# Stage joins, result stores, row buffers, load order and product order in an attention and MLP kernel

## The chip, the cores and the metric

One NeuronCore of a Trainium2 chip runs the whole program. The metric is the device time of one execution in microseconds. Engines are named PE (TensorE), PEld (its weight loads), DVE (VectorE), ACT (ScalarE), POOL (GpSimd) and SP (SyncE), which only issues transfers here.

## What is computed

```python
xn = layernorm(x)                                   # x is (16, 512, 128)
x + causal_attention(xn) + ffn(xn)

# causal_attention: 16 heads of 64, relative position bias, softmax, @ Wo + bo
# ffn: two layers, each
h = shift_token(x)                                  # second half of the features from the row before
q, k, v = split(h @ wqkv)                           # 8 heads of 64; l2norm, scales, rotary
x = x + local_attention(q, k, v) @ wo               # windows of 64, one window back
h = layernorm(shift_token(x)) * lg + lb
a, g = split(h @ w1 + b1)                           # 2 x 341
x = x + (a * gelu(g)) @ w2 + b2
```

All inputs and results are f32. Most products are made of three f32r passes (high and low parts of both operands).

## The kernel before

The normalised input and later the residual of `ffn` stay on chip in `xf` (64 tiles of 128 rows). There are 16 batches of 4 tiles.

`causal_attention` runs first: 16 batches times 8 pairs of heads, one slot (b, p) for each, with an order of work written out by hand for each engine. POOL scales the probabilities, ACT makes exponentials and copies, DVE adds the bias table and makes the low parts, PE multiplies and transposes. At p = 4 the next batch is transposed too (`transpose_x`, `xT_high` on ACT, `xT_low` on DVE), before k of the next pair is projected. Each finished batch is stored to `out` from SP's queue; the program waits for the last store.

`transformer` then opens a block of its own: SP loads the rotary table and layer 0's weights, the shifted rows of batch 0 (`load_shifted`, up to three copies a tile, chip to chip memory) and reads `out` back to `f_acc` (4 MB). POOL builds masks. Then comes a hardware loop over the two layers; its body is `local_attention` and `gated_mlp`, each a block whose engines meet at its end.

`local_attention` has 64 tiles, one slot (b, t) each, and a pipeline of up to five slots. It begins with DVE's split of `wqkv` and POOL's scaling of the tables (`f_tab`). In slot (b, t) SP waits until the place in `f_hs` is free, copies the tile's shifted rows, and then copies `f_v` of two tiles back to `f_vm`. PE transposes the rows (L1149) near the end of the same tile's slot; ACT makes `f_hT_hi` and DVE `f_hT_lo`. At the end SP copies the shifted rows of batches 0 and 1 for the MLP.

`gated_mlp` has 16 slots of a batch of 512 rows and three more to drain. SP starts with the next layer's attention weights, then copies each batch's shifted rows into one of two buffers with three copies (L745 to L747), after the batch two before has been normalised. In slot b DVE normalises batch b - 1, gates batch b - 2 (`gated(0)`), takes the statistics of batch b, adds the result of batch b - 3 to `xf` and gates twice more. PE makes the products of `w1` (`hidden`), the transposes, and the products of `w2` (`second`). POOL makes the reciprocal root and `hT_lo`. After its last slot SP copies the shifted rows of batch 0 for the next layer.

After the loop DVE adds `xf` to `f_acc` in four parts, and SP stores them.

Of the kernel before, what the change touches and what calls it, by code (L numbers as in the profile page):

```python
# [112 lines left out]
def causal_attention(nc, c, x, Wq, Wk, Wv, Wo, bo, rel, out, ext_dram):  # L113

    xf, ident, bank = c["xf"], c["ident"], c["bank"]
    with ExitStack() as ctx:
# [101 lines left out]
        def _(sp):  # L218
# [20 lines left out]
            def turn(b, par):  # L239

                if not isinstance(b, int) or b < B - 2:
                    sp.wait_ge(s_Ya, at(b, HP, 2))
                    sp.dma_start(xb[:, par], xv[:, bass.ds(b * TT + 2 * TT, TT), :]).then_inc(s_x[par], 16)
                for half in range(2):
                    sp.wait_ge(s_Ya, at(b, HP, 7 + half))
                    sp.dma_start(ov[:, bass.ds(b * TT + 2 * half, 2), :],
                                 yacc[:, 2 * half:2 * half + 2, :]).then_inc(s_out[half], 16)
            for b in range(B):
                turn(b, b % 2)
            for half in range(2):  # L250
                sp.wait_ge(s_out[half], 16 * B)

        @block.gpsimd
        def _(pool):
# [39 lines left out]
            def slot(b, p, par):  # L294
# [15 lines left out]
                if p == 4 and has_scores(b) and has_next(b):  # L310
                    keep(b + 1, 1 - par)
            pair_slots(pool, slot, 1)

        @block.scalar
        def _(act):
# [39 lines left out]
            def slot(b, p, par):  # L355
# [52 lines left out]
        def _(dve):  # L408
# [51 lines left out]
            def slot(b, p, par):  # L460
# [37 lines left out]
                logits(3, 0)  # L498
                if step is not None:
# [9 lines left out]
                if p == 4 and has_scores(b) and has_next(b):  # L509
                    xT_low(b + 1, 1 - par)  # L510
# [244 lines left out]
def load_attention_weights(eng, c, d, l, s):  # L755

    def row(a):
        return a[bass.ds(l, 1), :].to_broadcast([P, DH])
    eng.dma_start(c["wqkv"][:], d["wqkv"][bass.ds(l, 1), :, :].squeeze(0)).then_inc(s, 16)
    eng.dma_start(c["wo4"][:], d["wo"][bass.ds(l, 1), :, :].squeeze(0).rearrange("(c p) n -> p c n", p=P)).then_inc(s, 16)  # L760
    eng.dma_start(c["qk_scale"][:, 0, :], row(d["q_scale"])).then_inc(s, 16)
    eng.dma_start(c["qk_scale"][:, 1, :], row(d["k_scale"])).then_inc(s, 16)


def local_attention(nc, c, d, l, w):
# [17 lines left out]
    def _(sp):  # L783

        s = sem["weights"]
        sp.dma_start(c["w1"][:], d["w1"][bass.ds(l, 1), :, :].squeeze(0)).then_inc(s, 16)
        sp.dma_start(c["w2"][:, 0:2, :], d["w2"][bass.ds(l, 1), 0:2 * P, :].squeeze(0).rearrange("(c p) n -> p c n", p=P)).then_inc(s, 16)
        sp.dma_start(c["w2"][0:CH[2], 2, :], d["w2"][bass.ds(l, 1), 2 * P:HID, :].squeeze(0)).then_inc(s, 16)
        sp.dma_start(c["w2"][CH[2]:CH[2] + 1, 2, :], d["b2"][bass.ds(l, 1), :]).then_inc(s, 16)
        with nc.allow_non_contiguous_dma(reason="a few columns, once a layer"):  # L790
            sp.dma_start(c["ln"][:, 0:1], d["ln_g"][bass.ds(l, 1), :].rearrange("l p -> p l")).then_inc(s, 16)
            sp.dma_start(c["ln"][:, 1:2], d["ln_b"][bass.ds(l, 1), :].rearrange("l p -> p l")).then_inc(s, 16)
            for part in range(2):
                for j in range(3):
# [4 lines left out]
        def slot(b, t):
            if not isinstance(b, int) or 0 < b < B:  # L800
# [4 lines left out]
            if two is not None:  # L805
# [16 lines left out]
    def _(pool):  # L822
        for n in w["mlp"].values():
            pool.sem_clear(n)

        for k in range(4):
            nc.gpsimd.tensor_tensor(tab[:, :, k, :], w["rope"][:, :, k, :],
                                    c["qk_scale"][:, k // 2, :].unsqueeze(1).to_broadcast([P, TT, DH]),
                                    ALU.mult).then_inc(sem["tab"], 1)
# [4 lines left out]
        def slot(b, t):  # L834
# [21 lines left out]
            if one is not None:  # L856
# [6 lines left out]
                nc.gpsimd.tensor_tensor(rn[:, r, :], ssq[:, r, :], w["mhalf"][:], ALU.pow).then_inc(sem["rn"], 1)  # L863
        tile_slots(pool, slot)

    @block.scalar
    def _(act):
        def slot(b, t):
# [21 lines left out]
            def rotated_out(k):  # L890
# [620 lines left out]
```

## Time and profile before

| | |
|---|---|
| three runs | 2701.99, 2704.53, 2706.19 us |
| median | 2704.53 us |
| profiled execution | 2707.02 us |
| its span | 2705.2 us |
| PE, PEld busy | 2547.8 us (94%), 1988.1 us (73%) |
| ACT, DVE, POOL busy | 2158.3 (80%), 2009.4 (74%), 1629.7 us (60%) |
| mean granted clock of PE | 0.977 |
| transfers | 77.07 MB, mean 28 GB/s |

The span reaches from the first to the last instruction; the execution's own time lies around it. Busy shares are means over stages with different limits. In timelines "[2.81 <-DMA f_hs<-xf]" is the engine's idle time before the group and what ended it; "SPq" is SP's queue, and its duration that of issuing, not of the transfer.

### The profile page before, as it was taken

What the parts mean: (1) busy time and instruction counts of PE and PEld (TensorE: products, weight loads), DVE (VectorE), ACT (ScalarE), POOL (GpSimd) and SP (SyncE); (2) the same over time, 40 slices, a digit from 0 to 9 for tenths busy, and PEclk for the clock granted to TensorE, in tenths of its full rate; (3) what the DMA queues carried; (4) which work ended last, traced back from release to release, by engine and by line L of the source; (5) the groups of instructions that cost most, each with busy time, mean ns of one, the idle gap of its engine ahead of it and who ended that gap; (6) DMA issues with size and microseconds to landing.
All of it is one profiled execution on the core that took longest, in us unless ns stands there. A gap on an engine that the chain in (4) does not pass through costs nothing. (4 is left out here: it accounts for less than half of the span.)

```text
span 2705.2 us, 71234 instructions
## 1 busy us (share of the span) xinstructions
PE 2547.8 (94%) x24208; PEld 1988.1 (73%) x24208; DVE 2009.4 (74%) x5647; ACT 2158.3 (80%) x6335; POOL 1629.7 (60%) x1947
## 2 busy tenths in 40 slices
PE   7999999999999999999599999997979999999796
PEld 4777777777777777777378888885767888888575
DVE  4666666666666666666389999995659999999565
ACT  5888888888888888888389999996438999999642
POOL 3444444444444444444389999994229999999521
PEclk8999999999999999999799999998989999999898
DMA  2000000000000000000311111111111111111112
GB/s 72 7 7 10 9 9 5 8 7 9 9 9 5 10 7 7 9 6 5 103 41 41 38 42 39 38 42 46 33 26 40 38 42 42 38 40 42 46 33 79
DMA packets 128513, 77.07 MB, mean 28 GB/s; under 512 B 80196, under 2 KB 110736, under 8 KB 128144
## 3 DMA queue, kind: packets, MB, share of 16 engines
q1 hardware_dynamic: 127968, 72.34, 10.9%
q8 instruction: 199, 3.26, 0.5%
q14 instruction: 170, 1.39, 0.2%
q10 hardware_dynamic: 176, 0.07, 0.0%
HBM read 17.58 MB, written 8.41 MB: 10 GB/s over the span
## 5 line engine op out<-in xcount | busy, mean ns | idle before, releaser
L306 POOL TENSOR_SCALAR L<-L,rinv 128x128 f32<-128x128 f32 (+3 forms) x1024 | 522.4, 533 | 622.7 <-DVE rinv L488 622.7
L370 ACT ACTIVATE L<-L,nmax 128x384 f32<-128x384 f32 (+3 forms) x1024 | 571.8, 561 | 144.2 <-DVE nmax L474 144.2
L474 DVE CUSTOM_DVE_ANT_0 L<-bank,bias_tab 128x256 f32<-128x256 f32 (+3 forms) x1024 | 470.5, 479 | 180.3 <-PE bank L590 178.3
L886 ACT ACTIVATE f_L<-bank,f_nmax,f_rn 128x128 f32<-128x128 f32 x1024 | 459.9, 486 | 5.0 <-DVE f_nmax L1013 5.0
L863 POOL TENSOR_TENSOR f_rn<-f_ssq,f_mhalf 128x16 f32<-128x16 f32 x128 | 419.1, 3274 | 18.2 <-DVE f_ssq L997 4.7
L845 POOL TENSOR_TENSOR f_qkr<-f_ab 128x256 f32<-128x256 f32 x512 | 414.3, 838 | 10.3 <-DVE f_ab L964 10.3
L611 PE MATMUL bank<-ident,L 128*128 128x128 f32 x2560 | 370.4, 276 | 2.3 <-DVE PT L215 2.0
L611 PEld LDWEIGHTS bank<-ident,L 128*128 128x128 f32 x2560 | 296.8, 141 | 83.4 <-issue 46.1
L964 DVE TENSOR_TENSOR f_ab<-bank,f_tab 128x512 f32<-128x512 f32 x512 | 347.8, 680 | 8.8 <-ACT f_sq L876 8.8
L632 PE MATMUL bank<-PT,v 128*64 128x512 f32 (+3 forms) x2048 | 303.9, 439 | 0.6 <-DVE yacc L507 0.4
L632 PEld LDWEIGHTS bank<-PT,v 128*64 128x64 f32 x2048 | 126.8, 136 | 166.2 <-issue 164.9
L886 ACT ACTIVATION_READ_ACCUMULATOR f_L<-bank,f_nmax,f_rn 128x1 f32 x1024 | 239.6, 234 | 0.0
L215 ACT ACTIVATE PT<-bank 128x512 f32<-128x512 f32 x384 | 226.9, 591 | 6.2 <-PE bank L611 4.2
L443 DVE TENSOR_TENSOR k_lo<-bank,k_hi 128x512 fp32r<-128x512 f32 x128 | 88.5, 691 | 187.8 <-ACT k_hi L337 187.8
L215 DVE COPY PT<-bank 128x512 f32<-128x512 f32 x256 | 175.6, 686 | 36.1 <-PE bank L611 35.9
L370 ACT ACTIVATION_READ_ACCUMULATOR L<-L,nmax 128x1 f32 x1024 | 201.8, 197 | 0.0
L1050 PE MATMUL bank<-f_w_hi,f_hT_hi 128*128 128x512 f32 x384 | 188.1, 490 | 10.5 <-DVE f_hT_lo L1026 10.5
L988 DVE TENSOR_REDUCE f_rmax<-bank 128x4 f32<-128x512 f32 x256 | 164.8, 685 | 30.9 <-PE bank L1083 30.9
L590 PE MATMUL bank<-k_hi,q_hi 64*128 64x128 f32 (+3 forms) x1024 | 180.1, 348 | 6.3 <-DVE k_lo L443 5.3
L876 ACT ACTIVATE f_sq<-bank 128x512 f32<-128x512 f32 x256 | 174.2, 681 | 12.9 <-PE bank L1052 12.9
L978 DVE TENSOR_REDUCE f_ssum<-f_sq 128x8 f32<-128x512 f32 x256 | 169.5, 662 | 0.0
L590 PE MATMUL bank<-k_hi,q_lo 64*128 64x128 f32 (+3 forms) x1024 | 166.0, 320 | 0.0
(145 smaller groups left out, 6390.8 us busy)
## 6 DMA issues: line engine op xcount, KB each, us to landing
f_vm<-f_v SPq DMA_DIRECT2D x224, 128.0 KB, 2.4
f_hs<-xf SPq DMA_DIRECT2D x132, 32.0 KB
f_hs<-xf SPq DMA_DIRECT2D x132, 31.8 KB
xb<-in_L_attn_x SPq DMA_DIRECT2D x16, 256.0 KB, 2.8
out<-yacc SPq DMA_DIRECT2D x32, 128.0 KB, 1.8
f_hs<-xf SPq DMA_DIRECT2D x32, 128.0 KB
out<-f_acc SPq DMA_DIRECT2D x4, 1024.0 KB, 7.5
f_hs<-xf SPq DMA_DIRECT2D x32, 127.0 KB
```

The costliest lines, as they stand in the source:

```text
L215: copy(PT[:, k, 0:n], ps_t[(h + k) % 2][:, 0:n], *how).then_inc(s_C[engine], 1)
L306: nc.gpsimd.tensor_scalar(t, t, rinv[:, h % RING, a, i:i + 1], 1.0, ALU.mult, ALU.mult).then_inc(s_N, 1)
L370: nc.scalar.activation(t, t, ACT.Exp, bias=nmax[:, ep % RING, a, i:i + 1], scale=-1.0, accum_out=rsum[:, ep % RING, a, i:i + 1]).then_inc( ...
L474: nc.vector.tensor_tensor_reduce(out=L[:, p % RING, a, LOFF[i]:LOFF[i] + (i + 1) * P], in0=ps_s[a][i], in1=bias_tab[:, 2 * p + a, T - (i + ...
L590: last[a] = nc.tensor.matmul(ps_s[a][i], qq[row, r, tok], kk[row, r, keys], start=(n == 0), stop=(n == 2))
L611: last = nc.tensor.transpose(ps_t[(h + k) % 2][:, n * P:n * P + P], L[:, h % RING, a, LOFF[i] + j * P:LOFF[i] + j * P + P], ident[:])
L632: last = nc.tensor.matmul(ps_o[DH * a:DH * a + DH, j * P:T], v[:, j, head:head + DH], PT[:, fill, off:off + T - j * P], start=(j == 0), st ...
L845: nc.gpsimd.tensor_tensor(halves(qkr[:, tt % 2, k], s), halves(ab[:, tt % 2, k, 0], s), halves(ab[:, tt % 2, k, 1], 1 - s), ALU.add).then_inc(
L863: nc.gpsimd.tensor_tensor(rn[:, r, :], ssq[:, r, :], w["mhalf"][:], ALU.pow).then_inc(sem["rn"], 1)
L886: nc.scalar.activation(L[:, ot % 2, a, k, :], ps_s[a][:, k * P:k * P + P], ACT.Exp, bias=nmax[:, ot % 2, a, k:k + 1], scale=rn[:, ot % 2, ...
L964: ins = nc.vector.tensor_tensor(ab[:, it % 2, k, n, :].rearrange("p (h e) -> p h e", h=FH), src[:].rearrange("p (h e) -> p h e", h=FH), ta ...
L1050: nc.tensor.matmul(ps[:], hT_hi[:, it % 2, :], w_hi[:, col], start=True, stop=False)
```

## The change

Six things change.

1. *Joins.* `transformer_start` allocates part of the layers' tensors ahead of the causal attention; some of them are places in that stage's tensors (`f_rows` is its bias table). At (0, 6) POOL builds the masks; at b = 1 SP copies the shifted rows of batch 0; at b = 15, after pair 3, SP loads table and weights of layer 0; POOL scales and splits them at (15, 6), (15, 7) and (16, 0). The block between is gone; some fills open layer 0 on POOL. The loop over the layers is written out. In `local_attention` the first batch of the MLP is taken through statistics, scale, transposes and affine step, and `w1` is split, in the last slots. In the MLP of layer 0 POOL prepares the weights of layer 1.
2. *Results.* `out` is read back at slot (6, 0) of layer 0's attention. In the last MLP, POOL adds `xf` to `f_acc` batch by batch, DVE adds the batch's result to that, and ScalarE's queue stores it, 256 KB each, in the slot after.
3. *Buffers.* Four buffers for the MLP's shifted rows instead of two (two lie in `f_sq`). Batches 0 and 1 are copied at slots (4, 0) and (5, 0) of the attention.
4. *Loads.* In layer 0's MLP SP issues the next layer's tables and weights in slots 4 to 6 and the shifted rows of its batch 0 in slots 7 to 10. The last MLP loads nothing of that kind.
5. *Products.* PE does `hidden(0)`, `hidden(1)`, the transposes, all of `second`, `hidden(2)`. DVE adds the result after `gated(1)`.
6. *p = 4 of the causal attention.* ACT copies `v` before the exponential (2, 1); DVE makes `xT_low` before it adds to `yacc`.

```diff
 # causal_attention, SP
             def turn(b, par):
+                if b == B - 1:
+                    sp.wait_ge(s_L, at(b, 8 * HP, 8 * 4))
+                    for part in range(3):
+                        load_attention_weights(sp, c, d, w, 0, part, w["s_load"])
+                if b == 1:
+                    sp.wait_ge(s_xf, 1)
+                    sp.wait_ge(w["s_hs_zero"], 1)
+                    for t in range(TT):
+                        load_shifted(sp, c["hs"], xf, 0, t, w["attn"][f"hs{t}"])
...
 # causal_attention, POOL
+                if (b, p) == (0, 6):
+                    build_masks(nc, pool, c, w)
+                for n in {(B - 1, 6): (0, 1, 2), (B - 1, 7): (3, 4, 5), (B, 0): (6, 7)}.get((b, p), ()):
...
+                    prepare_attention(nc, pool, c, w, n, w["s_load"])
 # causal_attention, ACT
                 fills(1)
+                if p == 4 and item is not None:
+                    value_out(item)
                 exps(2, 1)
-                if item is not None:
+                if p != 4 and item is not None:
                     value_out(item)
 # causal_attention, DVE
                 logits(3, 0)
+                if p == 4 and has_scores(b) and has_next(b):
+                    xT_low(b + 1, 1 - par)
                 if step is not None:
...
-                if p == 4 and has_scores(b) and has_next(b):
-                    xT_low(b + 1, 1 - par)
                 logits(0, 0)

-def load_shifted_batch(sp, hs, xf, b, r, s_hs):
-    x_b = xf[:, bass.ds(b * TT, TT), :]
+def load_shifted_batch(sp, w, xf, b):
+    hs, s_hs = w["shifted"][b % 4], w["mlp"][f"hs{b % 4}"]
+    x_b = xf[:, b * TT:b * TT + TT, :]
     half = D // 2
-    sp.dma_start(hs[:, r, :, 0:half], x_b[:, :, 0:half]).then_inc(s_hs, 16)
-    sp.dma_start(hs[1:P, r, :, half:D], x_b[0:P - 1, :, half:D]).then_inc(s_hs, 16)
-    sp.dma_start(hs[0:1, r, 1:TT, half:D], x_b[P - 1:P, 0:TT - 1, half:D]).then_inc(s_hs, 16)
+    sp.dma_start(hs[:, :, 0:half], x_b[:, :, 0:half]).then_inc(s_hs, 16)
+    sp.dma_start(hs[1:P, :, half:D], x_b[0:P - 1, :, half:D]).then_inc(s_hs, 16)
+    sp.dma_start(hs[0:1, 1:TT, half:D], x_b[P - 1:P, 0:TT - 1, half:D]).then_inc(s_hs, 16)

+def load_attention_weights(eng, c, d, w, l, part, s):
+    if part == 0:
+        eng.dma_start(w["tab"], d["rope"].rearrange("(t p) k e -> p t k e", p=P)).then_inc(s, 16)
+    elif part == 1:
+        eng.dma_start(w["w_raw"], d["wqkv"][l]).then_inc(s, 16)
+    else:
+        # wo and two rows of scales
+def prepare_attention(nc, pool, c, w, n, s_loaded):
+    # n = 0..3: a quarter of the tables; 4..7: high and low parts of wqkv, 1024 and 512 columns
+def batch_statistics(nc, dve, w, b):      # as in the MLP before: bn_stats, bn_aggr, add epsilon
+def batch_scale(nc, pool, w, b):          # rstd
+def batch_normalise(nc, dve, w, b):       # hn
+def batch_transposes(nc, pe, c, w, b):    # four transposes to bank 6
+def batch_affine(nc, act, c, w, b):       # mT and mT_hi
+def batch_low(nc, pool, w, b):            # mT_lo

 # local_attention, SP, at the end of slot(b, t); the two loads after the slots are gone
+            if b in (4, 5) and t == 0:
+                sp.wait_ge(w["s_fill"], 4)
+                sp.wait_ge(sem["x_out"], 2 * TT)
+                load_shifted_batch(sp, w, xf, b - 4)
+            if (l, b, t) == (0, 6, 0):
+                sp.dma_start(w["acc"][:], d["out"].rearrange("b (t p) d -> p (b t) d", p=P)).then_inc(w["s_acc"], 16)
 # local_attention: DVE (B, 0) statistics of 0, (B, 2) normalise 0 and statistics of 1;
 # POOL (B, 1) scale, (B, 2) split of w1, (B + 1, 0) low; PE (B, 3) transposes; ACT (B + 1, 0) affine

 # gated_mlp, SP
-        load_attention_weights(sp, c, d, 1 - l, sem["weights"])
+        nxt = l + 1 if l < DEPTH - 1 else None
         def slot(b, r):
-            if isinstance(b, int) and (b < 2 or b >= B):
-                return
-            sp.wait_ge(sem["hn"], at(b, TT, -TT))
-            load_shifted_batch(sp, hs, xf, b, r, sem[f"hs{r}"])
+            if 2 <= b < B:
+                sp.wait_ge(sem["hn"], at(b, TT, -3 * TT))
+                load_shifted_batch(sp, w, xf, b)
+            if nxt is not None and 4 <= b < 7:
+                load_attention_weights(sp, c, d, w, nxt, b - 4, sem["weights"])
+            if nxt is not None and 7 <= b < 11:
+                sp.wait_ge(sem["x_out"], 1)
+                load_shifted(sp, c["hs"], xf, 0, b - 7, w["attn"][f"hs{b - 7}"])
 # gated_mlp, POOL
+            if l == DEPTH - 1 and now is not None:
+                pool.wait_ge(w["s_acc"], 16)
+                a = w["acc"][:, b * TT:b * TT + TT, :]
+                nc.gpsimd.tensor_tensor(a, a, xf[:, b * TT:b * TT + TT, :], ALU.add).then_inc(sem["acc"], 1)
 # gated_mlp, ACT, ahead of gelu(0)
+            four = batch_back(b, 4)
+            if l == DEPTH - 1 and four is not None:
+                act.wait_ge(sem["x_out"], four + 1)
+                act.dma_start(d["out"].rearrange("b (t p) d -> p (b t) d", p=P)[:, four * TT:four * TT + TT, :],
+                              w["acc"][:, four * TT:four * TT + TT, :]).then_inc(w["s_stored"], 16)
 # gated_mlp, PE
             hidden(0)
+            if two is not None:
+                pe.wait_ge(sem["H"], at(two, 3, -1))
+            hidden(1)
+            if one is not None and one > 0:
+                batch_transposes(nc, pe, c, w, one)
             if three is not None:
                 pe.wait_ge(sem["H"], at(three, 3, 3))
                 pe.wait_ge(sem["x_out"], at(three, 1, 0))
-                second(range(2))
-            # transposes of batch `one`
-            if three is not None:
-                second(range(2, TT)).then_inc(sem["y_done"], 1)
+                second()
             if two is not None:
                 pe.wait_ge(sem["H"], at(two, 3, 0))
-            hidden(1)
             hidden(2)
 # transformer
-        with nc.Fori(0, DEPTH) as l:
+        for l in range(DEPTH):
             local_attention(nc, c, d, l, w)
             gated_mlp(nc, c, d, l, w)
-        # a block before the loop (loads, masks) and one after it (four sums, four stores)
```

## Rows read from the trace of the kernel before

**Rows 1.** Windows by stage: start:end, us, busy of each engine, granted clock, DMA.
```profile
1315.60:1342.00 26.40, 0.52 (x2) 0.22 (x2) 5.32 (x6) 1.56 (x2) 7.71 (x16) 0.52 0.49 143
1342.00:1865.70 523.70, 511.47 (x6399) 424.00 (x6399) 479.47 (x1023) 493.12 (x1599) 481.44 (x384) 0.98 0.19 44
1865.70:2010.20 144.50, 123.77 (x736) 101.34 (x736) 81.14 (x272) 57.28 (x81) 39.08 (x34) 0.95 0.15 36
2010.20:2020.20 10.00, 0.47 (x1) 0.18 (x1) 3.58 (x3) 1.56 (x2) 4.28 (x4) 0.63 0.25 62
...
2685.70:2705.20 19.50, 0.00 (x0) 0.00 (x0) 8.92 (x5) 0.00 (x0) 0.00 (x0) 0.57 0.76 215
```

**Rows 2.** Timeline of the first join: start, us, engine, line, idle before it.
```profile
1315.13 0.42 DVE L507 TENSOR_TENSOR yacc<-bank,yacc 128x256 f32<-128x256 f32 x1 [1.31 <-PE bank L655]
1318.67 0.11 POOL L1411 MEMSET f_mhalf<- 128x16 f32 x1 [14.45 <-POOLq L116]
...
1339.01 0.48 PE L1149 MATMUL bank<-ident,f_hs 128*128 128x128 f32 x1 [23.92 <-DVE f_w_lo L942]
1339.53 0.28 ACT L913 ACTIVATE f_hT_hi<-bank 128x128 fp32r<-128x128 f32 x1 [2.02 <-PE bank L1149]
1341.62 0.29 DVE L1026 TENSOR_TENSOR f_hT_lo<-bank,f_hT_hi 128x128 fp32r<-128x128 f32 x1 [2.66 <-POOL f_tab L827]
...
1341.96 0.80 PE L1050 MATMUL bank<-f_w_hi,f_hT_hi 128*128 128x512 f32 x1 [2.47 <-DVE f_hT_lo L1026]
```

**Rows 3.** Timeline of the MLP, layer 0: SyncE's issues and the statistics.
```profile
1939.95 6.53 SPq L747 DMA_DIRECT2D f_hs<-xf  x1
...
1946.52 0.66 SPq L745 DMA_DIRECT2D f_hs<-xf  x1
...
1947.22 0.71 SPq L746 DMA_DIRECT2D f_hs<-xf  x1
...
1948.67 0.87 DVE L1265 BATCH_NORM_STATS2 f_stats<-f_hs 128x6 f32<-128x128 f32 x4 [2.81 <-DMA f_hs<-xf]
```

**Rows 4.** Timeline of the end.
```profile
2685.04 0.69 DVE L1276 TENSOR_TENSOR xf<-bank,xf 128x512 f32<-128x512 f32 x1 [3.04 <-PE bank L1302]
...
2688.55 9.66 SPq L1453 DMA_DIRECT2D out<-f_acc  x4
```

**Rows 5.** Timeline of the MLP's start, layer 0.
```profile
1874.21 0.66 SPq L745 DMA_DIRECT2D f_hs<-xf  x1
...
1875.39 0.78 ACT L1225 ACTIVATE f_mT<-bank,f_ln 128x512 f32<-128x512 f32 x1 [11.26 <-PE bank L1319]
...
1876.99 1.26 POOL L1202 TENSOR_TENSOR f_w_lo<-f_mT,f_w_hi 128x512 fp32r<-128x512 f32 x1 [3.96 <-ACT f_w_hi L1228]
```

**Rows 6.** Timeline of steady attention: a tile's rows, and the transpose using them.
```profile
1494.35 0.60 SPq L734 DMA_DIRECT2D f_hs<-xf  x1
...
1495.65 0.86 SPq L738 DMA_DIRECT2D f_hs<-xf  x1
...
1503.90 0.27 PE L1149 MATMUL bank<-ident,f_hs 128*128 128x128 f32 x1
```

**Rows 7.** Timeline of SyncE in the first join.
```profile
1334.04 0.85 SPq L1396 DMA_DIRECT2D f_acc<-out  x1
...
1336.39 11.52 SPq L786 DMA_DIRECT2D f_w<-in_L_ffn_w  x1
```

**Rows 8.** Timeline of a causal slot with p = 4.
```profile
707.51 0.40 PE L527 MATMUL bank<-wv_lo,xT_hi 128*128 128x512 f32 x1
...
707.95 0.60 ACT L345 ACTIVATE v<-bank 128x512 f32<-128x512 f32 x1
...
709.30 0.59 ACT L330 ACTIVATE xT_hi<-bank 128x512 fp32r<-128x512 f32 x1
...
710.52 0.68 DVE L437 TENSOR_TENSOR xT_lo<-bank,xT_hi 128x512 fp32r<-128x512 f32 x1
...
711.26 0.50 PE L525 MATMUL bank<-xT_hi,wk_hi 128*128 128x512 f32 x1 [0.68 <-DVE xT_lo L437]
```

More of the change, by code:

```diff
@@ L251, in _ @@
                 sp.wait_ge(s_out[half], 16 * B)
+            sp.wait_ge(w["s_load"], 16 * 5)
+            for t in range(TT):
+                sp.wait_ge(w["attn"][f"hs{t}"], shifted_count(t))
         @block.gpsimd
@@ new lines, in batch_statistics @@
+def batch_statistics(nc, dve, w, b):
+    sem, hs, stats, mv, ve = w["mlp"], w["shifted"][b % 4], w["stats"], w["mv"], w["ve"]
+    dve.wait_ge(sem[f"hs{b % 4}"], 48 * (b // 4 + 1))
+    for t in range(TT):
+        nc.vector.bn_stats(stats[:, t, :], hs[:, t, :]).then_inc(sem["stats"], 1)
+    dve.wait_ge(sem["stats"], at(b, TT, TT))
+    dve.wait_ge(sem["hn"], at(b, TT, 0))
+    dve.sem_inc(w["gate_dve"], 1)
+    for t in range(TT):
+        nc.vector.bn_aggr(mv[:, t, :], stats[:, t, :]).then_inc(sem["mv"], 1)
+    dve.wait_ge(sem["mv"], at(b, TT, TT))
+    nc.vector.tensor_scalar(ve[:], mv[:, :, 1], LN_EPS, None, ALU.add).then_inc(sem["ve"], 1)
@@ new lines, in batch_scale @@
+def batch_scale(nc, pool, w, b):
+    pool.wait_ge(w["mlp"]["ve"], b + 1)
+    nc.gpsimd.tensor_tensor(w["rstd"][:], w["ve"][:], w["mhalf"][:, 0:TT], ALU.pow).then_inc(w["mlp"]["rstd"], 1)
+def batch_transposes(nc, pe, c, w, b):
+    sem, ps_t = w["mlp"], c["bank"][6]
+    pe.wait_ge(sem["hn"], TT * (b + 1))
+    pe.wait_ge(sem["hT_hi"], b)
+    for t in range(TT):
+        last = nc.tensor.transpose(ps_t[:, t * P:t * P + P], w["hn"][:, t, :], c["ident"][:])
+    last.then_inc(sem["T_done"], 1)
@@ new lines, in batch_low @@
+def batch_low(nc, pool, w, b):
+    sem = w["mlp"]
+    pool.wait_ge(sem["hT_out"], b + 1)
+    pool.wait_ge(sem["hT_hi"], b + 1)
+    nc.gpsimd.tensor_tensor(w["mT_lo"][:, b % 2, :], w["mT"], w["mT_hi"][:, b % 2, :].bitcast(F32),
+                            ALU.subtract).then_inc(sem["hT_lo"], 1)
+def batch_normalise(nc, dve, w, b):
+    sem = w["mlp"]
+    dve.wait_ge(sem["rstd"], b + 1)
+    dve.wait_ge(sem["T_done"], b)
+    for t in range(TT):
+        nc.vector.tensor_scalar(w["hn"][:, t, :], w["shifted"][b % 4][:, t, :], w["mv"][:, t, 0:1], w["rstd"][:, t:t + 1],
+                                ALU.subtract, ALU.mult).then_inc(sem["hn"], 1)
@@ L822, in _ @@
     def _(pool):
[L823 to L829, printed above, removed]
+        if l > 0:
+            for n in w["mlp"].values():
+                pool.sem_clear(n)
+        else:
+            nc.gpsimd.memset(kT[:, :, 0:WIN], 0.0).then_inc(w["s_fill"], 1)
+            nc.gpsimd.memset(vm[0:WIN, 0, :], 0.0).then_inc(w["s_fill"], 1)
+            nc.gpsimd.memset(w["hs2"][:], 0.0).then_inc(w["s_fill"], 1)
+            nc.gpsimd.memset(w["Hh"][:, :, 2, :], 1.0).then_inc(w["s_fill"], 1)
         def halves(a, r):
@@ L1183, in _ @@
-        for t in range(TT):
-            sp.wait_ge(w["attn"][f"hs{t}"], shifted_count(t))
-        sp.wait_ge(sem["weights"], 64)
+            if 2 <= b < B:
[6 more added lines that the diff above has]
+                load_shifted(sp, c["hs"], xf, 0, b - 7, w["attn"][f"hs{b - 7}"])
@@ L1207, in _ @@
+            if now is not None and b > 0:
+                batch_scale(nc, pool, w, b)
+            if l < DEPTH - 1 and 7 <= b < 15:
+                prepare_attention(nc, pool, c, w, b - 7, sem["weights"])
+            if l == DEPTH - 1 and now is not None:
+                pool.wait_ge(w["s_acc"], 16)
+                a = w["acc"][:, b * TT:b * TT + TT, :]
+                nc.gpsimd.tensor_tensor(a, a, xf[:, b * TT:b * TT + TT, :], ALU.add).then_inc(sem["acc"], 1)
         batch_slots(pool, slot, 3)
@@ L1295, in hidden, with second @@
                     nc.tensor.matmul(ps[0:n, :], w1_hi[:, col], hT_lo[:, r, :], start=False, stop=True).then_inc(sem["ga_done"], 1)
-            def second(tiles):
-                for t in tiles:
+            def second():
+                for t in range(TT):
                     for j in range(3):
@@ L1310, in slot @@
             hidden(0)
+            if two is not None:
+                pe.wait_ge(sem["H"], at(two, 3, -1))
+            hidden(1)
+            if one is not None and one > 0:
+                batch_transposes(nc, pe, c, w, one)
             if three is not None:
@@ L1313, in slot @@
                 pe.wait_ge(sem["x_out"], at(three, 1, 0))
-                second(range(2))
-            if one is not None:
-                pe.wait_ge(sem["hn"], at(one, TT, TT))
-                pe.wait_ge(sem["hT_hi"], at(one, 1, 0))
-                for t in range(TT):
-                    last = nc.tensor.transpose(ps_t[:, t * P:t * P + P], hn[:, t, :], ident[:])
-                last.then_inc(sem["T_done"], 1)
-            if three is not None:
-                second(range(2, TT)).then_inc(sem["y_done"], 1)
+                second()
             if two is not None:
                 pe.wait_ge(sem["H"], at(two, 3, 0))
-            hidden(1)
             hidden(2)
```

312 lines of the change are left out of this document (151 added, 161 removed).

## The prediction

> **What bounds the kernel now.** I read the stretches between the stages' ends first [rows 1]. An attention layer (523.7 us) keeps PE 98% and ACT 94% busy. An MLP (144.5 us) does not: PE works 123.8 us, ACT 57.3, POOL 39.1. Three stretches hold almost no compute: 26.4 us between the causal attention and the first attention layer, 10.0 us between the layers, 19.5 us at the end.
>
> Then the timeline, to see what fills them. In the first join [rows 2] the last addition ends at 1315.55, the first transpose comes at 1339.01, held by DVE's split of the weights, and the first projection at 1341.96, since `hT_lo` stood in DVE's stream behind a wait for POOL's tables. In the MLP [rows 3] VectorE waits 2.81 us at `bn_stats` for a load. SyncE issues the three copies of a batch in 0.66, 0.71 and 6.53 us, and the next batch's first follows the third's end by 0.04 us: 1939.95 + 6.53 = 1946.48, then 1946.52. So SyncE doesn't wait for a free buffer there; it is full, and its 8.02 us a batch (third copy to third copy: 1939.95, 1947.97) are the MLP's cadence.
>
> **The joins.** *Causal attention to layer 0.* Weights, tables, masks and shifted rows are made earlier. The barrier stays: 3.12 us from the last addition to the next block's first instruction, 1318.67 [rows 2]. Then transpose to `hT_hi` 0.52, `hT_hi` itself 0.28, from `hT_lo`'s start to the projection 0.34, and 0.2 to start with: 1320.1. Gain 21.9 us (20 to 22.5). POOL's four fills there lie beside transposes, projections and DVE's products, before its first rotation; if that cover is gone they cost their 2.5 us or so, which is in the bound. The preparation that moves under the last pairs of the causal stage runs on POOL between its shares of those pairs; at the very tail I allow 0.4 us, an estimate.
>
> *Between the layers* [rows 1] 10.0 us become the same start and a table load of ACT, 2.5 us: gain 7.5 (6 to 8.5).
>
> *End.* The last addition ends at 2685.73, after which come 19.5 us of sums and four 1 MB stores [rows 1, 4]. One store of 256 KB remains. Store, landing and barrier of the causal stage took 3.12 us [rows 2]; with twice the bytes 3.2. Gain 16.3 (15 to 17). This execution took 2707.02 us, its span and 1.8 us, and is 2.5 us above the median of the runs; the difference is applied to the median, 2704.53.
>
> **The MLP stages.** The first load inside the MLP is issued at 1874.21 [rows 5], because it must wait for batch 0's `hn`; the stage began at 1865.7. With four buffers SyncE starts at once: 8.3 us earlier in each layer, 16.5 in both. That the first product also comes earlier does not count: from the third batch on `bn_stats` waits for SyncE. The form of the three copies is unchanged, so 14 batches still take 14 x 8.02 = 112.3 us. Before, 1874.21 + 112.3 + 2.2 of landing (1946.48 to 1948.67) is 1988.7, and the stage ended 21.5 us later; these are products of the last batches, the same number in the new order, so they stay. PE's 123.8/16 = 7.7 us a batch would be next, only 0.3 us below SyncE.
>
> Now what is added to that full stream. In layer 0 SyncE issues the next layer's loads inside slots 4 to 10. Four `load_shifted` take 2.16 us each (1494.35 to 1496.51 [rows 6]): 8 us. Weights and tables are 1.6 MB; four 1 MB stores took from 2688.55 to 2705.2 [rows 1, 4], 252 GB/s, by which these are 6 us of everything that copies, or 2 us if only issuing counts. I take 5: 13 us together (8 to 14). Before, they lay ahead of or behind the batches. In layer 1 twelve stores of 256 KB run before the last load lands; at that rate 1.04 us each. Only ScalarE's queue issues them, so either the copying is what is full (12 us) or SyncE's own time (0). I take 11 (0 to 12), since an issue of 6.53 us for the smallest of three copies [rows 3] reads as a queue that is held up by the copy before it.
>
> The Trainium skill (DMA: Bandwidth & Descriptors, "Why a DMA increments its semaphore by 16 and not by 1") says that 127 partitions put a whole copy on one DMA engine; the second copy of a batch has 127, and the trace's 6.53 us behind it agree. The same page ("Issuing engines are not separate DMA queues") speaks against the stores: another issuing engine brings no bandwidth. By it they cost their 11 us; if SyncE's time alone were the bound, 0, and the sum would be 2676.
>
> **New waits in the attention layers.** There the next tile's shifted rows are issued from 1494.35, the last of them until 1496.51, and transposed at 1503.90 [rows 6]. With 2.2 us of landing the slack is 5.2 us; PE and ACT are full, so what is later than that is lost. (a) The copies of MLP batches 0 and 1 now stand in SyncE's stream at slots (4,0) and (5,0), ahead of the next tile's rows: 8.0 us [rows 3] less 5.2 is 2.8 us, four times in two layers: 11 us (0 to 18). Behind the late rows stand PE's `values()`, ACT's `hT_hi` and with them all of the slot. (b) The 4 MB read of `out` moves to slot (6,0). Before, it was issued at 1334.04 and SyncE was stuck behind it until 1347.91, in an issue of 11.52 us [rows 7]: 13.9 us in place of the 0.60 of an issue, so 13.3 - 5.2 = 8.1 us lost once (2 to 12).
>
> **The rest.** Batch 0's statistics, transposes and affine step go into the attention's tail. After the last copy of `OT` ACT makes two steps of 0.78 us and POOL one of 1.26 [rows 5] before the barrier, partly beside the last product: 1.5 us a layer (1 to 2.5), 3 in all. The granted clock of PE was 0.52 in the first join [rows 1], that is the lower of its two levels, and full in the steady stage; with less idle time at the joins I give back 2 us (0 to 5). In the causal stage PE waits 0.68 us for `xT_lo` at p = 4 [rows 8], 15 times. `xT_lo` starts at 710.52 though `xT_hi` ended at 709.89, because the `yacc` addition stands first; moving it up is worth up to 0.6 us. But ACT's copy of `v` starts at 707.95, 0.04 us after PE's product (707.51 + 0.40), beside which an exponential of 0.6 us ran; pulled ahead of it the copy starts no earlier, and the exponential then delays `xT_hi`. The two cancel: 0 (-8.5 to +8).
>
> **The sum.** Gains 21.9 + 7.5 + 16.3 + 16.5 + 2 = 64.2. Losses 13 + 11 + 11 + 8.1 + 3 + 0.4 = 46.5. Net 17.7 us less: 2704.5 - 17.7 = 2686.8, say 2687.
>
> **Rivals.** *A: the new loads and stores are hidden.* Rows arrive in time and stores fit between. For it: copying is busy only 15 to 19% of the engines' time in these stages [rows 1]; against: SyncE's full cadence. Without 11 + 8 + 11 the net is -48, 2657; with half of it 2672. *B, on the other side: a long copy holds up the tile loads for its whole length.* If rows behind a batch copy come 9 us too late and those behind the read of `out` 16, that is 52 us instead of 19, and the net is +15: 2720. It decides from 37 us on, 7 us a batch copy with 9 for the read. For it: the third copy is held for 6.53 us; against: the batch copy after it starts without further delay. *C: four buffers free the MLP.* Then PE's 7.7 us set it: 28 x 0.3 = 8 us less, and 24 of the additions gone: 2655. *D: the joins don't shrink*, since a block starts as slowly unrolled as looped: the 7.5 and some 6 of the 21.9 are lost, 2700.
>
> **How the numbers follow.** My own sum, net -6 to -30: 0.55. A 0.20, C 0.07, B 0.10, D or a mixture near zero 0.08. Within 0.2%, 5.4 us, this measurement can hardly tell a change. Faster is 0.55 + 0.20 + 0.07 = 0.82, the same 0.08, slower 0.10. The range, 2662 to 2704, leaves out B and the far halves of A and C; the likeliest case's own is 2675 to 2699.
>
> **What would show it.** Right: the first projection near 1320; `bn_stats` still waiting for a load every 8.0 us, and every 9 in the second MLP; the transposes of `f_hs` late by 3 us at tiles 17 and 21 of each layer and by 8 at tile 25 of the first; 3 us after the last addition; PE's wait for `xT_lo` still there. Wrong: a third copy that is issued quickly, an MLP slot of 7.7 us, attention slots of 7.8 us throughout, or transposes late by more than 7 us each time.

## The result, and the profile after

The changed kernel takes 2709.73 us (median of 17 runs, 2706.78 to 2713.74), the kernel before 2704.53 in the same job: ratio 1.0019, 95% interval 1.0011 to 1.0026. The forecast was 2687 us. The change makes the kernel 5 us slower, just below what I had called the limit of telling; the interval lies wholly above 1.

The profiled execution after has a span of 2711.2 us. These are its windows by stage, with the columns of [rows 1].

```profile
1316.06:1320.96 4.90, 0.45 (x2) 0.19 (x2) 0.29 (x1) 0.28 (x1) 1.40 (x3) 0.58 0.19 43
1320.96:1872.92 551.96, 521.22 (x6403) 430.15 (x6403) 486.85 (x1045) 496.44 (x1601) 485.64 (x389) 0.96 0.19 45
1872.92:2025.30 152.38, 127.82 (x732) 102.64 (x732) 79.02 (x252) 54.22 (x79) 43.52 (x39) 0.96 0.16 37
2025.30:2026.83 1.53, 0.30 (x1) 0.14 (x1) 0.29 (x1) 0.28 (x1) 0.00 (x0) 0.99 0.24 23
2026.83:2565.93 539.10, 516.57 (x6403) 426.76 (x6403) 486.36 (x1045) 497.37 (x1602) 485.29 (x387) 0.97 0.17 39
2565.93:2708.50 142.57, 123.00 (x732) 100.53 (x732) 82.63 (x253) 54.22 (x79) 55.84 (x47) 0.98 0.21 54
2708.50:2711.20 2.70, 0.00 (x0) 0.00 (x0) 0.00 (x1) 0.00 (x0) 0.00 (x0) 1.00 0.33 97
```

Set beside the same stretches of before, with the prediction's terms put to the stage where they act:

| stretch, span us | before | after | measured | predicted |
|---|---|---|---|---|
| causal attention, to its last addition | 1315.56 | 1316.06 | +0.5 | +0.4 |
| first join, to the first projection | 26.40 | 4.90 | -21.5 | -21.9 |
| attention, layer 0, to its last addition | 523.71 | 551.96 | +28.3 | +15.1 |
| MLP, layer 0 | 144.51 | 152.38 | +7.9 | +4.8 |
| join between the layers | 10.05 | 1.53 | -8.5 | -7.5 |
| attention, layer 1 | 521.61 | 539.10 | +17.5 | +7.0 |
| MLP, layer 1 | 143.89 | 142.57 | -1.3 | +2.8 |
| end | 19.45 | 2.72 | -16.7 | -16.3 |
| clock given back | | | (in the rows) | -2.0 |
| sum | 2705.18 | 2711.22 | +6.0 | -17.7 |

The joins gave what was forecast: 46.7 us against 45.7. The attention layers took 45.8 us where 22.1 were forecast, and that is the miss. Their loss has three places. First, the slots behind a batch copy. SyncE's queue and PE's transpose of the tile's rows, in the timeline of the changed kernel (line 768 is the first copy of a batch, 770 the third, 756 the first of a tile):

```profile
1443.11 6.47 SPq L770 DMA_DIRECT2D f_hs<-xf  x1
1449.63 0.52 SPq L756 DMA_DIRECT2D f_hs<-xf  x1
...
1453.93 0.47 PE L1301 MATMUL bank<-ident,f_hs 128*128 128x128 f32 x1 [2.66 <-DMA f_hs<-xf]
```

And the 4 MB read (line 950) with the issue held behind it, the first copy of tile 25's rows:

```profile
1514.59 0.84 SPq L950 DMA_DIRECT2D f_acc<-out  x1
1515.49 14.15 SPq L756 DMA_DIRECT2D f_hs<-xf  x1
```

And windows from transpose to transpose: a normal slot, the one that ends with this wait, the two behind it, then the two after the 4 MB read.

```profile
1435.40:1443.26 7.86, 7.86 (x103) 6.54 (x101) 7.48 (x18) 7.70 (x27) 7.59 (x7) 1.00 0.20 47
1443.26:1453.93 10.67, 8.01 (x103) 6.46 (x101) 8.13 (x18) 8.29 (x29) 9.49 (x9) 0.97 0.18 42
1453.93:1464.54 10.61, 10.61 (x101) 8.84 (x101) 6.80 (x16) 7.35 (x23) 6.39 (x5) 0.71 0.15 34
1464.54:1472.28 7.74, 7.74 (x102) 6.50 (x101) 7.36 (x18) 7.69 (x27) 5.97 (x6) 1.00 0.19 43
...
1515.90:1533.78 17.88, 8.03 (x103) 6.46 (x101) 8.15 (x18) 8.29 (x29) 9.49 (x9) 0.85 0.91 248
1533.78:1543.77 9.99, 9.99 (x101) 8.42 (x101) 6.80 (x16) 7.34 (x23) 6.38 (x5) 0.75 0.13 31
```

The reader is to see two different losses of 2.8 us. In the second row PE works its usual 8.0 us and waits 2.7. In the third nothing waits, PE is busy for all of 10.61 us with the work that it does in 7.8 elsewhere: the granted clock is 0.71, which is the lower of its two levels for 6.3 us of that slot. A batch copy costs 2.8 + 2.8 us (1.45 instead of the second 2.8 where the low clock lasts 3.4 us), 9.8 a layer; the 4 MB read 10.0 + 2.2.

Second, the tail of the attention. DVE, POOL and PE there (894 is the normalisation of the MLP's batch 0, 841 the statistics of batch 1, 1148 the product that makes the last tile's probabilities, 1005 and 1007 the split of `w1`), and below it the view of line 894 alone:

```profile
1859.85 3.72 DVE L894 TENSOR_SCALAR f_hn<-f_hs,f_mv,f_rstd 128x128 f32<-128x128 f32 x4
1863.49 0.86 DVE L841 BATCH_NORM_STATS2 f_stats<-f_hs 128x6 f32<-128x128 f32 x4
...
1865.22 0.69 DVE L1148 TENSOR_TENSOR f_L<-f_L,f_rinv 128x512 f32<-128x512 f32 x1
...
1860.02 1.07 POOL L991 TENSOR_TENSOR f_L<-f_L,f_rinv 128x512 f32<-128x512 f32 x1 [4.92 <-DVE f_rinv L1099]
1861.03 0.75 POOL L1005 CAST f_w_hi<-f_w 128x682 fp32r<-128x682 f32 x1
1861.87 1.63 POOL L1007 TENSOR_TENSOR f_w_lo<-f_w,f_w_hi 128x682 fp32r<-128x682 f32 x1
...
1865.97 1.12 PE L1248 MATMUL bank<-ident,f_L 128*128 128x128 f32 x4 [4.18 <-DVE f_L L1148]
```

```profile
L894 DVE TENSOR_SCALAR f_hn<-f_hs,f_mv,f_rstd x4: 333/920/1786, 1859.9 to 1861.8; 128x128 f32<-128x128 f32 x4
```

Four operations of 0.33 us on a free DVE take 3.72; beside POOL's three the slowest takes 1.79. PE waits 4.18 us for a product that stands in DVE's stream behind them. In the kernel before, the wait for the same product was 0.71 us:

```profile
1858.90 0.93 PE L1096 MATMUL bank<-ident,f_L 128*128 128x128 f32 x4 [0.71 <-DVE f_L L1002]
```

From the last tile's transpose to the last addition the tail grew from 32.76 to 38.65 us and from 31.45 to 37.33: 5.9 in each layer.

Third, a steady attention slot is 7.852 us where it was 7.834: some 2 us in all.

In the second MLP a batch now takes 8.42 us, SyncE still without a gap. The rows that answer to [rows 3]:

```profile
2601.99 6.93 SPq L770 DMA_DIRECT2D f_sq<-xf  x1
...
2608.97 0.65 SPq L768 DMA_DIRECT2D f_sq<-xf  x1
2609.66 0.70 SPq L769 DMA_DIRECT2D f_sq<-xf  x1
...
2611.77 0.87 DVE L841 BATCH_NORM_STATS2 f_stats<-f_sq 128x6 f32<-128x128 f32 x4 [2.93 <-DMA f_sq<-xf]
```

### The profile page after: what moved, and what is told of

The parts are those of the page before. It is cut to its first block and busy times, and to the rows that moved or that the text cites. A ratio compares the mean times of both kernels' runs of the same rounds, so it can differ in the third digit from the quotient of the medians.

```text
span 2711.2 us, 71091 instructions
## 1 busy us (share of the span) xinstructions
PE 2567.7 (95%) x24208; PEld 1999.8 (74%) x24208; DVE 2005.6 (74%) x5640; ACT 2157.7 (80%) x6334; POOL 1662.2 (61%) x1974
## 5 line engine op out<-in xcount | busy, mean ns | idle before, releaser
L496 DVE CUSTOM_DVE_ANT_0 L<-bank,f_rows 128x256 f32<-128x256 f32 (+3 forms) x1024 | 469.7, 478 | 179.2 <-PE bank L612 177.3
L982 POOL TENSOR_TENSOR f_qkr<-f_rows 128x256 f32<-128x256 f32 x512 | 413.4, 837 | 28.3 <-DVE f_rows L1110 28.3
L1110 DVE TENSOR_TENSOR f_rows<-bank,f_rows 128x512 f32<-128x512 f32 x512 | 347.5, 679 | 16.4 <-ACT f_sq L1023 16.4
L991 POOL TENSOR_TENSOR f_L<-f_L,f_rinv 128x512 f32<-128x512 f32 x128 | 133.4, 1042 | 66.6 <-DVE f_rinv L1099 50.7
L1055 ACT ACTIVATE f_PT<-bank 128x512 f32<-128x512 f32 x256 | 139.4, 595 | 37.4 <-PE bank L1248 31.4
## 6 DMA issues: line engine op xcount, KB each, us to landing
f_hs<-xf SPq DMA_DIRECT2D x128, 31.8 KB
```

The source lines that it names most:

```text
L496: nc.vector.tensor_tensor_reduce(out=L[:, p % RING, a, LOFF[i]:LOFF[i] + (i + 1) * P], in0=ps_s[a][i], in1=bias_tab[:, 2 * p + a, T - (i + ...
L982: nc.gpsimd.tensor_tensor(halves(qkr[:, tt % 2, k], s), halves(ab[:, tt % 2, k, 0], s), halves(ab[:, tt % 2, k, 1], 1 - s), ALU.add).then_inc(
L1110: ins = nc.vector.tensor_tensor(ab[:, it % 2, k, n, :].rearrange("p (h e) -> p h e", h=FH), src[:].rearrange("p (h e) -> p h e", h=FH), ta ...
```

## The experiments

All but one start from the changed kernel. Times are medians; the ratio is to the kernel before on the same chip, and for comparison that of the changed kernel is 1.0019 (1.0011 to 1.0026).

### The 127-partition copy in two

```diff
-    sp.dma_start(hs[1:P, :, half:D], x_b[0:P - 1, :, half:D]).then_inc(s_hs, 16)
+    cut = P - 16
+    sp.dma_start(hs[1:cut + 1, :, half:D], x_b[0:cut, :, half:D]).then_inc(s_hs, 16)
+    sp.dma_start(hs[cut + 1:P, :, half:D], x_b[cut:P - 1, :, half:D]).then_inc(s_hs, 16)
```

(The counts that wait for a batch go from 48 to 64.)

> The changed kernel, but in each batch load the copy of 127 partitions (rows 1 to 127 of the second half) is issued as two copies, of 112 and of 15 partitions; one more DMA a batch, the bytes are the same. Theory: the 127-partition copy is served by too little of the DMA hardware, so that the third copy's issue (6.5 us on SyncE's queue in the profile of the changed kernel) stands behind it. Then that issue falls below 1 us, both MLPs run at TensorE's own pace (12 + 6 products of 0.23 us, 24 of 0.12, transposes: about 7.6 us a batch against 8.42 in the second MLP and 7.8 to 10.9 in the first), which gives about 20 and 10 us, and the late tiles 17, 18, 21 and 22 of the attention (10.7, 10.6, 10.6, 9.3 us against 7.86, in both layers) disappear, which gives about 18: near 2662 against 2710. Rival 1, the bytes or the number of pieces set it: one more issue of 0.7 us per batch and no gain, 2708 to 2720. Rival 2, SyncE's issues are relieved but something else holds the MLP at 8 us: only attention and the extra loads gain, about 30 us, 2680.

2649.5 us (2646.26 to 2650.52), ratio 0.9796 (0.9779 to 0.9812). The theory holds in all its places, and the gain of 60 us is larger than the 48 that I expected, chiefly because a batch of either MLP takes 7.28 us and not 7.6. SyncE's queue and the statistics in the second MLP (768, 770, 771, 772 are now a batch's four copies):

```profile
2559.47 0.68 SPq L768 DMA_DIRECT2D f_sq<-xf  x1
...
2560.19 0.66 SPq L770 DMA_DIRECT2D f_sq<-xf  x1
2560.89 0.90 SPq L771 DMA_DIRECT2D f_sq<-xf  x1
...
2561.83 0.74 SPq L772 DMA_DIRECT2D f_sq<-xf  x1
...
2567.30 0.86 DVE L843 BATCH_NORM_STATS2 f_stats<-f_hs 128x6 f32<-128x128 f32 x4
```

No issue is held, and the statistics no longer wait for a load (no bracket behind the row). The rates of DMA in 40 us of the second MLP, each number the mean of 1 us, first of the changed kernel (2600 to 2640 us), then of this one (2560 to 2600 us):

```profile
GB/s 25 45 117 18 18 18 18 220 62 36 138 23 18 18 18 108 176 25 83 78 18 18 18 18 241 41 37 137 23 18 18 18 156 126 19 117 43 18 18 18
```

```profile
GB/s 49 180 41 1 0 246 16 0 184 87 8 0 171 91 0 130 118 15 0 94 169 0 82 161 18 1 9 253 0 29 176 72 1 0 216 47 0 144 116 2
```

The plateaus of 18 GB/s, three or four microseconds long in every batch, are the 127-partition copy with nothing else beside it (with other transfers on top it lasts longer: 127 KB at 18 GB/s are 7.2 us). The next expectation misreads this row where it says that DMA moved 18 GB/s for 6.5 us of a batch: it is three or four, and the 6.5 us are the length of the held issue. With the cut they are gone. MLP stages: 124.8 and 123.1 us (152.4 and 142.6); attention: the late tiles 17, 18, 21 and 22 are at 7.8 or 7.9 us in both layers.

### Which cut: 113 + 14, and 126 + 1

The same edit with `cut = P - 15` and with `cut = P - 2`.

> As x1_copy_split, but cut at 113 and 14 partitions instead of 112 and 15. Theory 1: how a copy is spread over the 16 DMA engines hangs on whether its number of partitions can be divided (127 and 113 are prime, 112 = 16 x 7; the Trainium skill, page DMA: Bandwidth & Descriptors, has a rule of this kind). The sum goes by the trace: in the MLP of the changed kernel the DMA moved 18 GB/s for some 6.5 of every 8.4 us with a sixteenth of the engines busy. Then 113 partitions stay on one engine, 113/127 of 7.2 us = 6.4 us, an issue behind it on SyncE is still held for 5 us or more, tiles 17 and 21 stay late, a slot with extra loads stays above 8 us: 2665 to 2695. Theory 2: any cut into two smaller copies does it: 2649.5, as with 112 and 15.

> As x1_copy_split, but cut at 126 and 1 partitions. Theory 1 (the divisor; 126 = 14 x 9): nearly the whole copy is spread, over 14 engines: 2649 to 2653, as with 112 and 15. Theory 2 (the size of the largest piece counts): 126 partitions are as good as 127, nothing is gained and an issue is added: 2708 to 2720.

113 + 14: 2707.83 us, ratio 1.0002 (0.9986 to 1.0017). 126 + 1: 2648.51 us, ratio 0.9778 (0.9738 to 0.9819). One partition more in the first copy than in the cut above takes nearly the whole gain away, and a copy of 126 is as good as one of 112. So the size of the copy does not decide; the number's divisors fit. The view of line 771, the issue behind the copy of 113 partitions:

```profile
L771 SPq DMA_DIRECT2D f_sq<-xf x16: 5682/5782/7659, 1874.4 to 2673.1; - x16
```

Its median is 5.78 us, where the third copy of the changed kernel takes 6.6 to 6.9 and the same line behind 112 partitions 0.91. I had put the time of this kernel at 2665 to 2695; that was wrong, since the copy is 11% shorter but the issue added costs 0.75 us, and SyncE is as full as before (7.9 to 8.3 us a batch in the second MLP). The Trainium skill (DMA: Bandwidth & Descriptors, "Why a DMA increments its semaphore by 16 and not by 1") gives the largest number up to 16 that divides the partitions as the number of engines that share a copy; by it that is 1 for 127 and 113, 16 for 112, 14 for 126. The three cuts agree. They don't tell this rule from a simpler one, such as any even number, for which an odd number with divisors would have to be tried; but two engines for 126 partitions don't fit, since the rates with 126 + 1 show no plateau either.

### The kernel before with the same cut

```diff
-    sp.dma_start(hs[1:P, r, :, half:D], x_b[0:P - 1, :, half:D]).then_inc(s_hs, 16)
+    cut = P - 16
+    sp.dma_start(hs[1:cut + 1, r, :, half:D], x_b[0:cut, :, half:D]).then_inc(s_hs, 16)
+    sp.dma_start(hs[cut + 1:P, r, :, half:D], x_b[cut:P - 1, :, half:D]).then_inc(s_hs, 16)
```

> The kernel before with the split copy alone. Theory: the two MLPs of the kernel before were bound by the same copy (8.02 us a batch), not by TensorE, and two buffers are enough: they fall to the 7.28 us of the changed kernel with the split copy, 2 x 14 x 0.74 = 21 us: 2684. Then the change without the queue trouble is worth 2684 - 2649.5 = 34 us. Rival: with two buffers the load waits for the normalisation two batches back, and the load's whole time (three issues, landing) shows: 7.6 us or more a batch, 2692 to 2704.

2682.01 us (2680.91 to 2686.81), ratio 0.9924 (0.9910 to 0.9937). With two buffers a batch takes 7.29 us, so four are not needed for the cadence. The change itself is worth 32.5 us from here (2682.0 to 2649.5). Rival C (2655) took the buffers for what held the MLP. It was the copy: the changed kernel has the four buffers and took 2710 us, and that 2655 lies near the 2649.5 of the kernel with the cut is luck.

### The read of the output in pieces, and on another queue

```diff
-            if (l, b, t) == (0, 6, 0):
-                sp.dma_start(w["acc"][:], d["out"].rearrange("b (t p) d -> p (b t) d", p=P)).then_inc(w["s_acc"], 16)
+            if l == 0 and b < B and t == 1:
+                n = b * TT
+                sp.dma_start(w["acc"][:, n:n + TT, :],
+                             d["out"].rearrange("b (t p) d -> p (b t) d", p=P)[:, n:n + TT, :]).then_inc(w["s_acc"], 16)
```

> The changed kernel, but the 4 MB read of the output back into f_acc is 16 reads of 256 KB, one per batch, each at the second tile of the batch in the first layer's attention. Theory: the one long read holds the tile loads behind it (one attention interval of 17.9 us and one of 10.0 against 7.86), and 256 KB fit into the slack of a tile: 12 us less, 2697.5. Rival: the bytes cost what they cost wherever they are, each piece delays its tile by 0.75 us: 2709 to 2711.

2699.36 us, ratio 0.9981 (0.9972 to 0.9991). The first attention layer falls from 552.0 to 537.8 us, and the two long intervals are 7.9. The rival is out: the same bytes in pieces cost nothing.

The other kernel leaves the read whole, and at its place in the order, but has `act.dma_start` in place of `sp.dma_start`.

> The changed kernel with the 4 MB read in one piece at the same place, but issued by ScalarE and not by SyncE. Theory 1: the read held the tile loads because they stood behind it on SyncE's queue (one issue of 14.15 us after it), and the hardware behind both queues takes them in turns: the interval of 17.9 us falls to 9 or 10 and the time to 2698 to 2702. Theory 2: the read fills what both queues share, tile loads are late whoever issues it: 2708 to 2712.

2704.5 us, ratio 1.0002 (0.9992 to 1.0011): between the two. Timeline, ACT's issue (1081), SyncE's third copy of a tile (760), PE's transpose:

```profile
1524.29 0.86 ACTq L1081 DMA_DIRECT2D f_acc<-out  x1
...
1524.47 0.87 SPq L760 DMA_DIRECT2D f_hs<-xf  x1
...
1533.00 7.15 SPq L760 DMA_DIRECT2D f_hs<-xf  x1
...
1545.92 0.48 PE L1301 MATMUL bank<-ident,f_hs 128*128 128x128 f32 x1 [4.55 <-DMA f_hs<-xf]
```

The tile copy beside the read passes, and so do the next tile's first two; the third of the next tile is held for 7.15 us, where on SyncE's queue the very next issue was held for 14.15. PE waits 4.55 us instead of 9.85. But the hold ends at nearly the same distance from the read: 15.9 us after its issue here (1524.29 to 1540.15), 15.1 us in the changed kernel (1514.59 to 1529.64). So the other queue did not shorten what holds SyncE; it let five issues through first, and the one that is held came later. How much of the hold belongs to the queue itself this run doesn't show. The low clock behind the wait costs 2.9 us (2.2 in the changed kernel).

### The order of the tail

```diff
-            if (b, t) == (B, 2):
+            if (b, t) == (B, 3):
                 batch_normalise(nc, dve, w, 0)
                 batch_statistics(nc, dve, w, 1)
```

> The changed kernel, but the normalisation of batch 0 and the statistics of batch 1 stand one slot later in VectorE's order, behind the product of the last tile's probabilities. Theory: in the attention's tail TensorE waits 4.2 us for that product, which is queued behind 3.72 us of normalisation and 1.5 us of statistics; with the order changed about 4 of the 5.9 us that each tail has grown by come back, once in each layer: 2702. Rival, the normalisation is only late elsewhere (TensorE's transposes of its result then end later by as much, before the same last addition): 2708 to 2712.

2701.75 us, ratio 0.9990 (0.9981 to 1.0000). The tails are 34.89 and 33.77 us (38.65 and 37.33); PE's wait of 4.18 us for the product is 0.71:

```profile
1859.85 0.69 DVE L1148 TENSOR_TENSOR f_L<-f_L,f_rinv 128x512 f32<-128x512 f32 x1
...
1863.09 1.11 DVE L894 TENSOR_SCALAR f_hn<-f_hs,f_mv,f_rstd 128x128 f32<-128x128 f32 x4
...
1860.59 0.66 PE L1248 MATMUL bank<-ident,f_L 128*128 128x128 f32 x4 [0.71 <-DVE f_L L1148]
```

Behind POOL's work the four operations take 1.11 us together, 0.34 each. The remaining 2.2 us a tail are open. Two things lie in them whose shares no run separates: the added work (four transposes on PE, 0.66 us, and the steps around them), and a granted clock that is still lower than before, 0.90 against 0.95 in layer 0's tail and 0.95 against 1.00 in layer 1's.

### Without the stores

The issue in ScalarE's stream is made only for the last batch (`four == B - 1`), so 15 of 16 batches of the output are not written. ScalarE's waits ahead of these stores go with them.

> The changed kernel, but 15 of the 16 batches of the result are not stored (only the last one is), so that its output is not the reference's. Theory: the stores and their waits on ScalarE's queue are what makes a batch of the second MLP 8.42 us where one without extra loads took 7.8 to 8.1 in the first: about 0.45 x 13 = 6 us less, 2704. Rival: SyncE's three issues (0.66 + 0.7 + 6.6, and gaps) set 8.42 and the stores are hidden: no change, 2709 to 2711.

2705.64 us, ratio 1.0002 (0.9993 to 1.0012). A batch of the second MLP takes 8.08 us on average instead of 8.42, the stage 138.35 instead of 142.57: the stores, with those waits, cost 4.2 us. In the kernel with the cut nothing of that is seen: its second MLP, with stores, takes the same 7.28 us a batch as its first.

### All three together, and half of the reorder at p = 4

The cut at 112 + 15, the read in 16 pieces and the tail's new order, in one kernel.

> The changed kernel with three edits together: the 127-partition copy of a batch split in 112 and 15, the read of the output in 16 pieces, the tail's order on VectorE. If they add up: 2649.5 - 14 (attention of the first layer with the pieces: 537.8 us against 552.0) - 7.3 (tails 3.8 and 3.6 us shorter) = 2628. If the pieces of the read cost the same again once the copies no longer hold the queue, or the tail's 4 us are given back at the start of a faster MLP: 2635 to 2642.

2625.66 us (2624.86 to 2628.54), ratio 0.9714 (0.9701 to 0.9727). They add up, 2 us better than the sum. On top of it:

```diff
-                if p == 4 and item is not None:
-                    value_out(item)
                 exps(2, 1)
-                if p != 4 and item is not None:
+                if item is not None:
                     value_out(item)
```

> The kernel x5_three with ScalarE's order in slot p = 4 of the causal attention put back (the value copy after the exponentials), VectorE's move left in. The step in the prediction gave VectorE's move alone 0.57 us less in each of 15 slots (11.57 us now), 8.5 us less than x5_three, and ScalarE's move the same in the other direction. Rival: what ends last in that slot is TensorE's wait for another of the two, and the slot stays at 11.6: no change.

2615.0 us (2613.35 to 2616.73), ratio 0.9673 (0.9660 to 0.9686), 10.7 us less. The causal slot of p = 4, from copy of `v` to copy of `v`, falls from 11.59 us in the changed kernel to 10.98; 15 such slots give 9.2 of the 10.7 us. ACT and DVE in such a slot, and PE's wait, first in the changed kernel, then in this one:

```profile
710.00 0.59 ACT L350 ACTIVATE xT_hi<-bank 128x512 fp32r<-128x512 f32 x1
...
710.62 0.69 DVE L459 TENSOR_TENSOR xT_lo<-bank,xT_hi 128x512 fp32r<-128x512 f32 x1 [1.14 <-ACT xT_hi L350]
...
711.37 0.19 PEld L547 LDWEIGHTS bank<-xT_hi,f_wk_hi 128*128 128x128 f32 x1 [0.93 <-DVE xT_lo L459]
```

```profile
704.48 0.60 ACT L350 ACTIVATE xT_hi<-bank 128x512 fp32r<-128x512 f32 x1
...
705.11 0.69 DVE L457 TENSOR_TENSOR xT_lo<-bank,xT_hi 128x512 fp32r<-128x512 f32 x1 [0.55 <-ACT xT_hi L350]
...
705.85 0.19 PEld L545 LDWEIGHTS bank<-xT_hi,f_wk_hi 128*128 128x128 f32 x1 [0.33 <-DVE xT_lo L457]
```

In the kernel before, `xT_hi` started 1.79 us after the start of PE's last product for the values (707.51, 709.30 [rows 8]); in the changed kernel it is 2.38 us (707.62, 710.00), an exponential of 0.6 us later, which takes back what DVE's new order gives. This is the version to keep: 3.3% under the kernel before.

## Why the prediction was wrong, step by step

**Right, in size too.** The first join (21.9 forecast, 21.5 measured), the end (16.3, 16.7), the join between the layers (7.5, 8.5), the causal stage as a whole (0.4, 0.5) and the reorder at p = 4 (0 for the pair, 0.02 us a slot measured, and 8.5 for DVE's part alone, where the last experiment measured 0.61 x 15 = 9.2 in the slots). The view of what bounds the MLP was right as well: SyncE's three issues, `bn_stats` waiting for each load, and the 127-partition copy behind them, which the three cuts show. PE's own pace of 7.7 us a batch was too long, though: with the copy cut in 112 and 15 a batch takes 7.28 or 7.29 in both kernels, so rival C's 0.3 us a batch should have been 0.7.

**"2.8 us, four times in two layers: 11 us."** The wait was right (PE waits 2.55 to 2.66 us, the slot is 2.7 to 2.8 longer); the step failed in counting nothing behind it. Each wait is followed by a stretch of lower granted clock, and since PE is busy for all of a slot this costs 0.44 us per microsecond of low clock: 2.76 us for 6.3, 1.45 for 3.4. The four copies measured 19.6 us. It followed each of the five waits of the changed kernel. In the kernel with the cut at 113 it was absent once, behind tile 21 of layer 0, and there the next slot took 7.8 us. Where the copies are cut at 112 both losses go.

**"13.3 - 5.2 = 8.1 us lost once."** The wait was 9.85 us, as SyncE was held for 14.15 + 0.84 and not 13.9, which made the slot 10.0 us longer, and 2.2 us of low clock came behind it: 12.2.

**"1.5 us a layer (1 to 2.5)."** This is the step that failed outright: 5.9 a layer. I counted ACT's and POOL's steps at the very end and gave DVE's no place in its stream. Its normalisation and statistics, 5.2 us, stand ahead of a product that PE waits for, and the change puts the split of `w1` on POOL just beside them. Moving the two recovered 3.7 of the 5.9 us; what the other 2.2 are stays open.

**"So the 14 batches still take 14 x 8.02", and the start.** The gain at the MLP's start was 6.5 us in each layer and not 8.3. The third batch's statistics begin 12.2 us after the last addition (1872.92 to 1885.14), where it was 18.7: the block starts 1.9 us after that addition, through a barrier that I had left out. The loads in layer 0 cost 14.8 us from the third batch's statistics to the last (13 forecast), and layer 1 grew there by 5.4 us (11 for the stores), of which 4.2 are the stores themselves; the rest is that a batch takes 8.08 us even without them, where it took 7.99 before. I had weighed that either all copying or SyncE's time alone is full, and took a value near the first end. It lies between: a store lengthens the held issue behind the 127-partition copy from 6.62 to 6.93 us. That one DMA engine is what is full, and that only a part of a store falls on it, would explain the size; it was only argued.

**The rivals.** B, the slower side, came in the time (2720 forecast, 2710 measured) and in part of its mechanism. Its threshold, 37 us of waits in place of 19, was met nearly: 19.6 + 12.2 = 31.8, and the tail's 8.8 us beyond the forecast did the rest. But the rows behind a copy were 2.8 us late and not 9; it was the clock that doubled the loss. A is out as it stood: of its three terms the waits cost 31.8 us and the loads and stores 20.2, so none was hidden, though the stores cost only half of what I had put. D is out, the joins shrank.

The miss is 23.7 us of span: copies 8.6, read 4.1, tails 8.8, MLP start 3.4, layer 0's loads 1.8, clock not gained as a sum of its own 2.0, steady slots 2.2; less 5.6 for the stores; the remaining 1.6, also a gain, are what joins, end and the first slots of the layers gave beyond the forecast.

**Open.** Why a steady attention slot is 0.018 us longer in each kernel with the change. Its instructions are the same, several of its tensors lie elsewhere; this wasn't tried.

## What to carry to other kernels

Where a queue's issue of a small copy takes microseconds, look at the shape of the copy before it: 127 partitions cost here what 112 + 15 or 126 + 1 don't, and mending that was worth 22 us without the rest of the change and 60 with it. On an engine that is full, price a stall as the wait and the low clock behind it. And whoever moves work ahead into a pipeline's tail should look at each engine's order, what is queued behind the moved work and which engine works beside it, and not at its duration elsewhere.

## What the hardware showed that I had not expected

- A wait of PE of 2.6 us brought 3.4 or 6.8 us at the lower clock in each of four cases of the changed kernel (0.6 us of the 6.8 lie in the end of the wait, 6.3 in the slot behind it); the next slot paid 1.45 or 2.76 us for it. In the wait of 9.85 us the low clock began 5.3 us before the wait's end. Once, with the cut at 113, a wait of 2.86 us brought none.
- DVE's `tensor_scalar` between SBUF tensors took 0.34 us alone and 1.06, 0.78 and 1.78 us beside POOL. POOL's instructions end at 1861.08, 1861.79 and 1863.49, and DVE's at 1861.16, 1861.87 and 1863.57: each ends just behind one of POOL's, as if it had to wait for it. The Trainium skill (SBUF — State Buffer, "Who interferes with whom") says that VectorE, in the modes that use both of its ports, and GpSimd lock a shared port pair against each other for a whole instruction, and that `tensor_scalar` can enter such a mode; the ends in the trace agree.
- A read of 4 MB moved to another issuing queue still held the first queue's small copies, and until 15.9 us after its issue, where it was 15.1 us on the same queue; only the issues in between went through.
